# Two fused transformer layers: spare PSUM banks for gate and up, early splits of layer-1 weights, and orders that count DVE and POOL as one port

## What is computed

```python
x = x + _L0_xattn_ref(_layernorm(x), ctx, ...)   # softmax over a normalised 512x512 similarity
x = x + _L0_ffn_ref(_layernorm(x), ...)          # dense gated FFN (2048) + 8 experts (256 each), top 2, four RMS norms
x = x + _L1_xattn_ref(_layernorm(x), ctx, ctx, ...)  # 16 heads, 4 kv heads, rope, causal
x = x + _L1_ffn_ref(_layernorm(x), ...)          # silu-gated FFN, 512 -> 2048 -> 512
```

## Time and profile before

| | us |
|---|---|
| median of 3 runs | 1860.8 |
| lowest, highest | 1858.88, 1864.35 |
| the profiled execution | 1861.49 |
| its span, first to last instruction | 1859.6 |
| PE busy with matmuls | 1702.2 (92%) |
| DVE, ACT, POOL busy | 1142.7, 801.1, 238.6 |
| mean granted clock | 0.959 |

### The profile page before, as it was taken

How to read it: one execution, slowest core, us unless ns; L and a number is a source line. 1 busy time by engine, 2 the same in 40 slices (tenths; PEclk the granted TensorE clock), 3 DMA queues, 4 the chain that set the end, 5 groups by cost and what they waited for, 6 DMA issues and landing times.

```text
span 1859.6 us, 27270 instructions
## 1 busy us (share of the span) xinstructions
PE 1702.2 (92%) x9460; PEld 1355.9 (73%) x9460; DVE 1142.7 (61%) x2444; ACT 801.1 (43%) x1791; POOL 238.6 (13%) x237
## 2 busy tenths in 40 slices
PE   3688997999988998799999999887999999999998
PEld 2577776888888986577667668666776778678887
DVE  5798688755565747974666665798466553543222
ACT  3565553334665742324555554442264551431111
POOL 1213226411121204210000001311000000000000
PEclk8698998999999999899999999888999999999999
DMA  3325456898798897769245327987952546245562
GB/s 104 113 103 179 155 163 244 293 351 283 251 307 309 275 338 282 269 235 304 63 141 160 86 70 267 361 322 274 310 169 61 171 130 215 80 140 195 196 215 93
DMA packets 125864, 384.87 MB, mean 207 GB/s; under 512 B 14497, under 2 KB 29217, under 8 KB 119969
## 3 DMA queue, kind: packets, MB, share of 16 engines
q1 hardware_dynamic: 118944, 360.59, 57.1%
q0 software_dynamic: 6784, 22.55, 3.5%
HBM read 278.75 MB, written 104.33 MB: 206 GB/s over the span
## 4 chain that ended last, share of the span: by engine, by line
PE 62%; DVE 17%; DMA 8%; issue 6%; ACT 4%; SPq 1%; POOL 1%; ACTq 0%; DVEq 0%; POOLq 0%
PE ps L1178 17%; PE ps L1180 16%; PE ps L1179 16%; PE ps L1332 5%; DMA raw<-in_ffn_w 4%; PE ps L1341 3%; DMA gu<-w_dram 2%; PE ps L1324 2%; PE ps L1184 2%; DVE gu L1678 2%; DVE act L1663 1%; DVE wd L1678 1%; ACT hid L1389 1%; DVE yb L1903 1%; PE ps L1325 1%
## 5 line engine op out<-in xcount | busy, mean ns | idle before, releaser
L1178 PE MATMUL ps<-xT,gu 128*128 128x512 f32 (+1 forms) x1392 | 535.2, 384 | 72.5 <-DVE act L1663 36.5
L1180 PE MATMUL ps<-xT,gu 128*128 128x512 f32 (+1 forms) x1392 | 514.6, 370 | 0.0
L1179 PE MATMUL ps<-xT,gu 128*128 128x512 f32 (+1 forms) x1392 | 514.0, 369 | 0.0
L1178 PEld LDWEIGHTS ps<-xT,gu 128*128 128x128 f32 x1392 | 271.3, 195 | 125.5 <-DVE act L1663 43.0
L1180 PEld LDWEIGHTS ps<-xT,gu 128*128 128x128 f32 x1392 | 269.8, 194 | 43.7
L1179 PEld LDWEIGHTS ps<-xT,gu 128*128 128x128 f32 x1392 | 271.2, 195 | 36.3
L1178 PE MATMUL ps<-wd,hid 128*128 128x512 f32 x604 | 249.6, 413 | 15.6 <-DVE acc L1698 9.0
L1179 PE MATMUL ps<-wd,hid 128*128 128x512 f32 x604 | 239.3, 396 | 0.0
L1180 PE MATMUL ps<-wd,hid 128*128 128x512 f32 x604 | 239.1, 396 | 0.0
L1389 ACT ACTIVATE hid<-act 128x512 fp32r<-128x512 f32 (+1 forms) x174 | 99.9, 574 | 299.6 <-DVE act L1663 298.4
L1663 DVE TENSOR_TENSOR act<-act,ps 128x512 f32<-128x512 f32 (+1 forms) x174 | 106.8, 614 | 151.1 <-PE ps L1180 150.4
(11 more groups left out here) (279 smaller groups left out, 2300.5 us busy)
## 6 DMA issues: line engine op xcount, KB each, us to landing
gu<-w_dram SPq DMA_DIRECT2D x160, 512.0 KB
raw<-in_ffn_w SPq DMA_DIRECT2D x94, 768.0 KB
wd<-w_dram SPq DMA_DIRECT2D x80, 512.0 KB, 5.4
w_dram<-gu SPq DMA_DIRECT2D x32, 1024.0 KB
w_dram<-wd SPq DMA_DIRECT2D x32, 512.0 KB
QT<-q_dram SPq DMA_DIRECT2D x48, 256.0 KB, 5.7
y_dram<-x SPq DMA_DIRECT2D x23, 512.0 KB
wcs<-tab_dram SPq DMA_DIRECT2D x16, 512.0 KB, 5.9
```

What stands on the lines that cost most here:

```text
L1178: mm(out_ap, ah, bh, start=start, stop=False)
L1179: mm(out_ap, ah, bl, start=False, stop=False)
L1180: return mm(out_ap, al, bh, start=False, stop=stop)
```

## The change

1. **Spare banks.** New functions gate_bank and up_bank send the gate and up of odd tiles to banks 4 and 5 in E, (0,2), (1,0) and (1,3). Even tiles, and all tiles of the other stages, stay on 0 and 1. The planner also makes "gate" follow "low" of two tiles before, which the ACT code waits for already.
2. **Early splits.** The tiles of (1,0) are no longer raw or kept. Their 48 pieces are loaded one by one by POOL's queue (eload, 256 KB each) into three slots of 512 KB cut from the raw buffers, rounded by ACT and subtracted by DVE (esplit), and stored to w_dram by SP (estore, 512 KB). A slot's next load waits for its store. The first load is held behind gate0 of tile 94, the first of (0,3). Tiles of (1,0) then load as "pre".
3. **Port-aware orders.** The planner books the DVE and POOL items listed in SHARED on a common timeline "PORT" as well, so that no two of them overlap in the plan. No instruction is changed by this, only the lists.
4. **x2store** (16 stores of 256 KB of the mid results) moves from SP's queue to POOL's.

```diff
     def is_raw(s):
-        return MAIN[s][0] == "E" or MAIN[s][1:3] in ((0, 0), (0, 1), (1, 0))
+        return MAIN[s][0] == "E" or MAIN[s][1:3] in ((0, 0), (0, 1))
     def is_kept(s):
-        return MAIN[s][0] == "F" and MAIN[s][1:3] in ((0, 1), (1, 0))
+        return MAIN[s][1:3] == (0, 1) and MAIN[s][0] == "F"
+    def gate_bank(s):
+        return 4 if s % 2 and (MAIN[s][0] == "E" or MAIN[s][1:3] in ((0, 2), (1, 0), (1, 3))) else 0
+    def up_bank(s):
+        return gate_bank(s) + 1
+    SHARED = {("DVE", kind) for kind in ("ctx", "kv", "bet", "resid", "xt", "low", "w", "wo", "esplit", "comb", "parts", "final", "qrow", "split", "weights", "top2", "places", "before")}
+    SHARED |= {("POOL", kind) for kind in ("gam", "xh", "xt", "parts", "qsum", "kprep", "kscale", "qtab")}
...
+        if kind == "gate":
+            return [("low", a[0] - 2)] if a[0] > 1 else []
...
+            "eload": lambda: [("estore", b - 3)] if b > 2 else [("w", LAST_EXPERT, 2)], "esplit": lambda: [("eload", b)], "estore": lambda: [("esplit", b)],
...
+        if item == ("eload", 0):
+            return [("gate0", FIRST["F", 0, 3])]
...
+        def reserve_port(engine, kind, t, us):
+            while True:
+                t, n = reserve(engine, kind, t, us)
+                start, m = reserve("PORT", None, t, us)
+                if start == t:
+                    busy["PORT"].insert(m, (t, t + us, None))
+                    return t, n
+                t = start
...
-                        t, n = reserve(engine, kind, t, us)
+                        t, n = (reserve_port if (engine, kind) in SHARED else reserve)(engine, kind, t, us)
...
+                elif kind == "estore":
+                    n = a[0]
+                    sp.wait_ge(early_low, n + 1)
+                    load(w_dram[1][n // 3][:, n % 3, :, :].bitcast(F32), early[:, n % 3, :, :]).then_inc(wd_stored[n % 3], 16)
...
+                elif kind == "eload":
+                    n = a[0]
+                    if n < 3:
+                        pool.wait_ge(w_low, PIECE["w", LAST_EXPERT, 2])
+                    else:
+                        pool.wait_ge(wd_stored[n % 3], early_store(n - 3))
+                    fetch(early[:, n % 3, 1, :], ffn_w_in[2 * HT + n // 3][:, n % 3, :]).then_inc(early_loaded[n % 3], 16)
+                elif kind == "x2store":
+                    b, i = a
+                    pool.wait_ge(finaled, nth("final", b, i))
+                    fetch(x2_dram[b][:, i, :], xm[:, i, :]).then_inc(x2_stored[i // 2], 16)
...
+                elif kind == "esplit":
+                    n = a[0]
+                    act_.wait_ge(early_loaded[n % 3], 16 * (n // 3 + 1))
+                    if n > 2:
+                        act_.wait_ge(wd_stored[n % 3], early_store(n - 3))
+                    func(early[:, n % 3, 0, :].bitcast(F32R), early[:, n % 3, 1, :], ACT.Copy).then_inc(early_high, 1)
...
+                    tt(out=piece[:, 1, :].bitcast(F32R), in0=piece[:, 1, :], in1=piece[:, 0, :], op=ALU.subtract).then_inc(early_low, 1)
```

More of the change, by code:

```diff
@@ L278, in steps @@
             "split": [("ACT", 0.53), ("DVE", 0.6)], "project": [("PE", 2.85), ("DVE", 0.6)], "rown4": [("ACT", 0.71)], "rowt4": [("PE", 0.36), ("ACT", 0.48), ("DVE", 0.6)],
-            "rn2": [("DVE", 1.5), ("PE", 2.0), ("ACT", 0.5)]}.get(kind, [])
+            "eload": [("POOL", 0.8)], "esplit": [("ACT", 0.53), ("DVE", 0.6)], "x2store": [("POOL", 0.8)], "rn2": [("DVE", 1.5), ("PE", 2.0), ("ACT", 0.5)]}.get(kind, [])
     def builds_on(item):
@@ L407, in banks @@
         if kind == "gate0":
-            return (0,)
+            return (gate_bank(a[0]),)
         if kind == "up0":
-            return (1,)
+            return (up_bank(a[0]),)
         return ()
@@ L422, in merge @@
         end, holder, downs, placed = {}, {}, [1], []
-        busy = {"ACT": [], "DVE": [], "POOL": [], "SP": [], "DMA": []}
+        busy = {"ACT": [], "DVE": [], "POOL": [], "SP": [], "DMA": [], "PORT": []}
         tensor, now, last_of = [], [0.0], {}
@@ L539, in merge @@
         return placed, orders
-    SIDES = [[[("raw", r)] for r in range(2, len(RAW))], *([[("pre", s, m)] for s in PRE] for m in range(3)), [[("wstore", s)] for s in KEPT], [[("wostore", j)] for j in range(2)],
+    SIDES = [pieces_of("eload", 3 * HT), pieces_of("esplit", 3 * HT), pieces_of("estore", 3 * HT)]
+    SIDES += [[[("raw", r)] for r in range(2, len(RAW))], *([[("pre", s, m)] for s in PRE] for m in range(3)), [[("wstore", s)] for s in KEPT], [[("wostore", j)] for j in range(2)],
              [[("dstore", g, t)] for g in range(len(GROUPS)) for t in range(group_tiles(g))], split_ticks(), expert_ticks(), [[("xtload", b)] for b in range(1, B)]]
@@ L588, in two_layers, with early_store @@
     GU_STORES, WD_STORES = loads_of(KEPT, 2), loads_of(KEPT, 3)
+    def early_store(n):
+        return 16 * sum(1 for s in KEPT if s % 3 == n % 3) + 16 * (n // 3 + 1)
     ctx = ExitStack()
@@ L605, in two_layers @@
         raw = sb("raw", [P, 2, 3, D])
+        early = raw[:, :, :, :].rearrange("p a m d -> p (a m) d").rearrange("p (r k) d -> p r k d", k=2)
         gu = sb("gu", [P, 2, 2, 2, D], F32R)
@@ L768, in two_layers @@
         exp_asked, exp_taken, both_ready, ranks_done, slots_ready = sems("exp_asked", "exp_taken", "both_ready", "ranks_done", "slots_ready")
+        early_high, early_low = sems("early_high", "early_low")
+        early_loaded = sems("early_loaded0", "early_loaded1", "early_loaded2")
         hot_ready, spotted = sems("hot_ready", "spotted")
@@ L916, in _ @@
                     from_ = w_dram[f][h][:, m, :, :].bitcast(F32)
-                    if m < 2:
+                    if f:
+                        sp.wait_ge(wd_stored[m], early_store(3 * h + m))
+                    elif m < 2:
                         sp.wait_ge(gu_stored[kept % 2], GU_STORES[kept])
@@ L996, in _ @@
                     load(wcs[:, i % 2, :, :], tab_dram[i]).then_inc(tab_loaded[i % 2], 16)
-                elif kind == "x2store":
-                    b, i = a
-                    sp.wait_ge(finaled, nth("final", b, i))
-                    load(x2_dram[b][:, i, :], xm[:, i, :]).then_inc(x2_stored[i // 2], 16)
                 elif kind == "qstore":
@@ L1188, in quarter @@
                 q, cols = x_slot(s), columns(s)
-                return three(ps[:, m, 0:width(s)], gu[:, s % 2, m, 0, rows(d)], gu[:, s % 2, m, 1, rows(d)],
+                return three(ps[:, gate_bank(s) + m, 0:width(s)], gu[:, s % 2, m, 0, rows(d)], gu[:, s % 2, m, 1, rows(d)],
                              xT[:, q, 0, d, cols], xT[:, q, 1, d, cols], d == 0, d == KD - 1)
@@ L1374, in _ @@
                     if mode(s) == "table":
-                        func(o, z, ACT.Silu if MAIN[s][1] else ACT.Gelu_apprx_tanh).then_inc(free[0], 1)
+                        func(o, z, ACT.Silu if MAIN[s][1] else ACT.Gelu_apprx_tanh).then_inc(free[gate_bank(s)], 1)
                     elif mode(s) == "tanh":
@@ L1654, in _ @@
                     s = a[0]
-                    o, z = act[:, s % 2, :], ps[:, 0, :]
+                    o, z = act[:, s % 2, :], ps[:, gate_bank(s), :]
                     dve.wait_ge(tanh_ready, TANH[s])
-                    stt(out=o, in0=o, scalar=1.0, in1=z, op0=ALU.add, op1=ALU.mult).then_inc(free[0], 1)
+                    stt(out=o, in0=o, scalar=1.0, in1=z, op0=ALU.add, op1=ALU.mult).then_inc(free[gate_bank(s)], 1)
                 elif kind == "mult":
@@ L1661, in _ @@
                     dve.wait_ge(up_done, nth("up", s))
-                    dve.wait_ge(free[0], use(0, "gate", s))
-                    tt(out=act[:, s % 2, 0:W], in0=act[:, s % 2, 0:W], in1=ps[:, 1, 0:W], op=ALU.mult).then_inc(free[1], 1)
+                    dve.wait_ge(free[gate_bank(s)], use(gate_bank(s), "gate", s))
+                    tt(out=act[:, s % 2, 0:W], in0=act[:, s % 2, 0:W], in1=ps[:, up_bank(s), 0:W], op=ALU.mult).then_inc(free[up_bank(s)], 1)
                 elif kind == "low":
@@ L1678, in _ @@
                     tt(out=of[:, 1, :], in0=raw[:, r % 2, m, :], in1=of[:, 0, :].bitcast(F32), op=ALU.subtract).then_inc(w_low, 1)
+                elif kind == "esplit":
+                    n = a[0]
+                    dve.wait_ge(early_high, n + 1)
+                    piece = early[:, n % 3, :, :]
+                    tt(out=piece[:, 1, :].bitcast(F32R), in0=piece[:, 1, :], in1=piece[:, 0, :], op=ALU.subtract).then_inc(early_low, 1)
                 elif kind == "wo":
```

14 lines of the change are left out of this document (7 added, 7 removed).

## The result

The changed kernel takes **1856.2 us** in the median (1846.6 to 1860.1, 20 runs) against 1861.9 for the kernel before (20 runs): ratio 0.9963, interval 0.9953 to 0.9974. It is faster by 5.7 us, clear of noise, and 29 us above the forecast of 1827. The profiled execution took 1854.3 us (span 1852.5), 7.2 less than the one of before.

What follows compares the result with a forecast made beforehand. PE is busy 92% of the span; after start-up its losses sit mainly in (0,2) and (1,0), where DVE is the bound. Terms -18 - 18 + 8 - 3 - 3 = -34 from 1861.5 give 1827 us, range 1798 to 1857.

Steps and rivals of the forecast that it cites:

- What bounds the kernel: PE's idle time and clock loss by stage: (0,2) and (1,0) sore after start-up, DVE the bound there; E loses 19 us.
- Spare banks in (0,2), -18: In (0,2), a mult may be a tile late: 12 us of waits and 6 of lost clock saved.
- Early splits, taken from (1,0), -18: In (1,0), split and mult waits end, -26 with clock; +6 for bank swaps and +2 for x2stores against it.
- The swap of banks 4 and 5 with the scores, +6: In (1,0), tiles 111 and 113 share banks with moved scores, exposing exp or mult to PE: +6 us.
- Early splits, put into (0,3), +8: In (0,3), a busier DVE costs 3 us and the three-slot ring delaying exps and mults costs 5.
- E, -3: In E, the spare banks bear on 4.6 + 3.1 us of waits on gelu and mult: -3 us.
- Port-aware orders, -3 in (0,0) and (0,1): In (0,0) and (0,1), planning DVE and POOL apart on the shared port saves 3 us for both stages.
- ring near its limit: Rival, 0.17: landings in (0,3) take 2.5 us more, some 15 us more are exposed, about 1845 us.
- ring rules: Rival, 0.08: landings of 12.7 us make (0,3) grow by up to 85 us, about 1905 us, slower than before.
- DVE stays the bound: Rival, 0.12: banks only shift the wait in (0,2); it gives 4 and (1,0) 10, about 1849 us.
- the change does nothing: Rival, 0.04: moved work brings back in (0,3) and early (1,0) what it frees, 1860 us.

Runs made afterwards that it cites:

- c_rawtwo: Kernel before plus the spare banks alone, with each raw weight of E but the first two tiles' as two loads: 1842.9 us (0.9903).
- b_port02: The change with the planner's port rule used only from the first tile of (0,2) on: 1859.4 us (0.9987).
- c_spread: The change with rows, tables and wd pieces held back in the load order of (1,0), nothing left out: 1850.4 us (0.9943).
- a_noport: The change planned without the shared port, so only the orders differ: 1856.0 us (0.9972).
- b_smallraw: The change with E's tiles loading only a quarter of each raw weight, the rest stale: 1840.3 us in its one run.
- b_banksonly: Kernel before with the spare banks alone; no early splits, no port rule, x2store on SP: 1855.0 us (0.9965).
- d_portboth: The change with c_spread's load order in (1,0) and c_rawtwo's two-load raw weights in E, port rule kept: 1839.4 us (0.9890).
- c_npspread: The change with c_spread's load order in (1,0) but without the port rule of the plan: 1843.5 us (0.9902).

## Why the prediction was wrong, point by point

- **In short**: two steps failed. I counted the waits that the early splits end in (1,0) at their full length, without the next-latest thing, and I priced the port rule for (0,0) and (0,1) alone, while it changed every stage. The terms were also added up stage by stage, and what one stage gained the next gave back more than once.
- **What bounds the kernel**: right for (0,2) and (1,0), and incomplete for E. I put E's 19 us down as small waits on gelu and mult and did not ask what ACT waited for there: 29.9 us on raw weights. c_rawtwo took 13 us out of that stage with two loads for one.
- **Spare banks in (0,2), -18**: the stage gave 16.1, waits on the mult are gone, the clock rose from 0.95 to 0.98. The size is right by luck, the reason is not. With the banks alone (0,2) gave nothing, since the late mult then holds the downs; in the change without them the stage was 147.1 us. It is 143.6 to 147.1 us in every kernel with both the port rule (from (0,2) on, at least) and the early splits, and 155.8 to 162.4 in every other: the orders of the plan shorten this stage. What they save there can be lost again further on, as in b_port02. The banks are worth 18 us of the time in the change and 7 alone.
- **Early splits, taken from (1,0), -18**: the stage lost 42.0 us before and 37.3 after, -4.7. This is the step that failed. "The wait on the split, 11.3 us, has no source any more" was true, and I counted its length as gained without asking what was next late. The next was in the same sum: "gains 48 pre loads; it issues each in well under 1 us and isn't late". They land behind 2 to 4 MB of others, 11.3 us of waits on them came in place of the split's 11.3, and one issue took 3.62 us. A raw weight of before has slots of its own: in the stage of before it was issued ahead of the start of the tile two before it for 10 of 14 tiles, by 1 to 20 us. A stored gate piece is issued only when that tile's gate is done, 3 to 7 us after its start, so that a landing of 10 to 16 us shows. Behind it came DVE: with the waits on loads down to 1.4 us, c_spread still loses 33.6 us here. Where the attention stayed in (0,3) (a_noport) the term came true and (1,1) took 8.9 us back; that the moved attention is what costs the rest in the change is likely, and no run tests it alone. The swap of banks 4 and 5 with the scores, +6, did not show: PE waited 1.6 us on the exp (1.0 and 0.6 us in two groups) in the stage.
- **Early splits, put into (0,3), +8**: measured +5.6 (28.2 to 33.8). The size is about right, the reason is not: the largest wait is one on a stored piece, 7.2 us, which the sum hadn't. The DMA share rose to 0.90. The ring of three slots was hardly felt: ACT stood for a landing twice, 3.9 us in all. POOL's 256 KB loads landed after 5.3 us in the median, as the earlier trace rows and not as the earlier trace rows; the 2.6 us of the Trainium skill's page "DMA: Bandwidth & Descriptors", section "Anatomy of one DMA — SWDGE (gpsimd) path", was not reached at 299 GB/s. PE's wait in (0,3), what ended ACT's idle time before the early split, and from the list of DMA issues (queue, size, median us to landing) the loads:

```profile
PE ps L1226 <- DMA gu<-w_dram: 7.2, 1, 7.2
...
  DMA raw<-in_ffn_w: 3.9, 2
...
raw<-in_ffn_w POOLq DMA_DIRECT2D x48, 256.0 KB, 5.3
```

- **E, -3**: +8, the second step that failed. The waits on gelu and mult are gone, yet with the banks alone E took 245.9 us, no less than before: the landing of the raw weights came next. On top the orders that the port rule gives there cost 5 to 8 us. That they do so by way of the raw slots is likely, not shown: where the waits on raw weights are gone (b_smallraw) E takes 236.2 us in spite of the rule, but ACT's waits on raw weights tell little, 34.4 us with the rule and 29.7 (a_noport) and 32.9 (b_banksonly) without. I had priced that rule for (0,0) and (0,1) alone, though it changes the orders of every stage. Why its order is worse, instruction by instruction, I have not tested.
- **Port-aware orders, -3 in (0,0) and (0,1)**: -2.8. The size is right: (0,0) took 191.2 to 192.0 us in the eight kernels with the rule from the start, and 194.6 to 196.6 in all others. Over the whole kernel the rule costs 0 (a_noport), 3 (d_portboth, not clear of noise) or 7 us (c_npspread).
- **(1,1)**, which I left at 0, lost 3.3 us more.
- Sum over the lost time of the stages from (0,0) to (1,1): -2.8 + 8.0 - 15.4 + 5.6 - 4.7 + 3.3 = -6.0, against -34. Of the 28 us missed, 11 are E and 13 are (1,0).
- **Rivals**: "ring near its limit" and "ring rules" fell with the 3.9 us. (By its own terms the first gives 1827 + 15 = 1842, not 1845.) "DVE stays the bound" came true in (0,2) for the banks alone; its time, 1849, is 7 us off. Nearest is "the change does nothing", 1860, which had 0.04: its mechanism came true for the early splits, +5.6 in (0,3) against -4.7 in (1,0). Direction and range were right, the size was not, and the range's end of 1857 held the result by less than 1 us.

## What to carry to other kernels

A wait that is taken away is worth the distance to the next-latest thing, not its own length: list for every waiting instruction the second releaser too. Loads moved from a ring with a long lead to one with a short lead need a place in the queue ahead of loads without haste, whatever the mean DMA share of the stage says (0.63 here, 1.03 in the 20 us that counted). Where a plan is made anew, price it in all stages, and judge a part by the time of the whole kernel: what it gives in one stage can be gone in the next.
